# Three stage joints in a fused transformer kernel: inputs fetched in the stage before, a store wait moved, region fills split over two queues

## What is computed

```python
def reference(...):
    x = x + ssm_block(layernorm(x))       # silu/sigmoid gate, scan over 1024 steps, rms norm, projection
    x = x + moe(layernorm(x))             # 8 experts, 2 for each token, 256 -> 512 -> 256, relu
    qkv = einsum('bsi,oi->bso', layernorm(x), W_qkv); Q, K = rope(Q), rope(K)
    attn = softmax(where(causal, Q @ K.T / sqrt(16), -inf)); x = x + (attn @ V) @ W_o.T   # 16 heads of 16
    x = x + moe2(layernorm(x))            # 16 experts, 2 for each token, and a shared one
    return x
```

## Time and profile before

| | us |
|---|---|
| runs, median (lowest to highest, 3) | 1679.52 (1676.56 to 1681.55) |
| the profiled execution | 1680.78 |
| its span, first to last instruction | 1679.1 |
| PE busy in the span | 1507.6 (90%) |
| DVE busy | 1016.9 (61%) |
| ACT busy | 735.6 (44%) |
| POOL busy | 575.4 (34%) |

### The profile page before, as it was taken

The page is one execution under the profiler, slowest core; times in us unless marked ns, Lnnn a source line. Parts: engine busy times, 40 slices in busy tenths (PEclk is TensorE's granted clock), DMA queues, the critical chain, the costliest instruction groups (busy, mean ns, idle before and its releaser), DMA issues. The chain is left out here.

```text
span 1679.1 us, 31220 instructions
## 1 busy us (share of the span) xinstructions
PE 1507.6 (90%) x9903; PEld 1136.5 (68%) x9903; DVE 1016.9 (61%) x3465; ACT 735.6 (44%) x1537; POOL 575.4 (34%) x995
## 2 busy tenths in 40 slices
PE   5999999983999999599599999999999597489988
PEld 3777777772999999456366666666666376368877
DVE  3345555443344444389598888888887275545558
ACT  3444444420222222245157777777777232244420
POOL 4123333344222222135623322333223164635520
PEclk9999999985999999799799999999999887789999
DMA  7001111013877777567956666666661485745556
GB/s 229 1 26 42 48 46 51 33 51 112 236 210 210 216 214 210 171 229 244 218 72 92 92 91 96 96 92 92 92 92 42 131 261 161 175 133 158 160 163 195
DMA packets 150592, 221.74 MB, mean 132 GB/s; under 512 B 23648, under 2 KB 98144, under 8 KB 150304
## 3 DMA queue, kind: packets, MB, share of 16 engines
q1 hardware_dynamic: 128672, 170.59, 44.1%
q0 software_dynamic: 13344, 36.55, 6.2%
q10 hardware_dynamic: 8416, 12.60, 2.5%
HBM read 141.16 MB, written 78.25 MB: 131 GB/s over the span
## 5 line engine op out<-in xcount | busy, mean ns | idle before, releaser
L1958 ACT ACTIVATE t_probs<-t_ps_st 128x512 f32<-128x512 f32 x576 | 313.2, 597 | 125.2 <-PE t_ps_st L2010 122.7
L1939 DVE CUSTOM_DVE_ANT_0 whole_sum<-t_ps_s,t_later 128x512 bf16<-128x512 f32 (+3 forms) x512 | 285.6, 587 | 16.6 <-PE t_ps_s L1996 14.6
L1915 POOL TENSOR_SCALAR_AFFINE_SELECT t_probs<-t_probs 128x128 f32<-128x128 f32 x512 | 137.4, 300 | 333.1 <-ACT t_probs L1958 331.4
L1996 PE MATMUL t_ps_s<-t_ks,t_qs 96*128 96x512 f32 (+3 forms) x768 | 247.6, 362 | 0.5 <-ACT t_neg_max L1951 0.5
L2010 PE MATMUL t_ps_st<-t_qs,t_ks 128*128 128x512 f32 (+3 forms) x768 | 242.7, 365 | 1.1 <-ACT t_probs L1958 0.8
L2010 PEld LDWEIGHTS t_ps_st<-t_qs,t_ks 128*128 128x128 f32 x768 | 136.8, 189 | 74.1 <-ACT t_probs L1958 40.7
L1939 DVE CUSTOM_DVE_ANT_0 whole_sum<-t_ps_s,t_later,t_first_max 128x512 bf16<-128x512 f32 (+3 forms) x256 | 140.5, 549 | 47.7 <-PE t_ps_s L1996 47.7
L2025 PE MATMUL t_ps_o<-t_probs,t_vs 128*17 128x256 f32 (+1 forms) x2560 | 154.9, 361 | 0.5 <-ACT whole_sum L1965 0.5
L1996 PEld LDWEIGHTS t_ps_s<-t_ks,t_qs 96*128 96x128 f32 x768 | 138.7, 190 | 17.6 <-DVE t_first_max L1939 1.3
L1381 PE MATMUL m_ps_h<-m_xt,m_w_t 128*128 128x128 f32 x1136 | 140.1, 277 | 0.0
L1351 POOL DMA_INDIRECT outputs_dram<-m_y,m_place x71 | 68.1, 959 | 208.2 <-DVE m_place L1426 200.5
(11 more groups left out here) (324 smaller groups left out, 2697.3 us busy)
## 6 DMA issues: line engine op xcount, KB each, us to landing
m_w_t<-in_w_dram SPq DMA_DIRECT2D x71, 512.0 KB, 4.4
t_qs<-qkt_dram SPq DMA_DIRECT2D x124, 128.0 KB, 5.2
t_ks<-qkt_dram SPq DMA_DIRECT2D x124, 128.0 KB, 5.6
m_x_t<-gathered_dram SPq DMA_DIRECT2D x79, 128.5 KB, 2.1
m_x_t<-gathered_dram SPq DMA_DIRECT2D x71, 129.0 KB, 2.2
d_ye<-outputs_dram SPq DMA_DIRECT2D x8, 1024.0 KB, 8.0
qkt_dram<-d_hi ACTq DMA_DIRECT2D x32, 256.0 KB, 5.1
qkt_dram<-d_lo SPq DMA_DIRECT2D x32, 256.0 KB, 6.7
```

Of the source, the lines that this page charges most:

```text
L1915: nc.gpsimd.affine_select(out=diag, in_=diag, compare_op=ALU.is_ge, fill=0.0, base=0, pattern=[[1, P]], channel_multiplier=-1).then_inc(ma ...
L1939: nc.vector.tensor_tensor_reduce(out=seen[:, (NP * p + x) % (RS + 1), 0:keys], in0=bank_of(p, x)[:, 0:keys], in1=masks, scale=1.0, scalar= ...
L1958: nc.scalar.activation(probs[:, p % 2, i // NST, base:base + STC], ps_st[(NX * p + i) % RT][:], ACT.Exp, scale=HD ** -0.5).then_inc(exp_re ...
L1996: nc.tensor.matmul(bank_of(p, x)[:, 0:keys], q[0:MAX_ROW, head, qc * P:(qc + 1) * P], k[0:MAX_ROW, head, k0:k0 + keys], start=True, stop=T ...
```

## The change

1. The weights, the rope table and x of the first two groups are loaded by SP at the end of its list in the experts' stage (`load_qkv_start`). Their buffers are made before that stage; rope lies in the last rows of `total`.
2. In `project_qkv` SP no longer waits for the stores of q and k. That wait stands in `attention` in two places: before ACT's first exponential and before SP's load of pair 8. The semaphores live outside the stages.
3. The loads of the first pair of heads move from ACT, tick 8, to SP, tick 6.
4. For group 7, DVE and not POOL adds the second two sums (`add_last`).
5. Six leading dummy matmuls in attention become three.
6. In `back` the fills of the first eight regions stay with SP, the other eight go to ACT, after its exponentials (`close_regions`).

```diff
                 fetch(t)
+            fetch_next(sp)
 
...
 
-def project_qkv(nc, sb, pb, sem, c, x_dram, outputs, kept, total, sum_dram, w_qkv_dram, rope_dram, qkt_dram, vs, fetch):
+def group_rows(dram, g):
+    return dram[bass.ts(g, 4 * P), :].rearrange("(j p) n -> p j n", p=P)
+
+
+def load_qkv_start(eng, c, total, x1_dram, w, w_qkv_dram, rope, rope_dram):
+    eng.dma_start(w[:], w_qkv_dram.rearrange("(k p) n -> p k n", p=P)).then_inc(c["w_loaded"], 16)
+    eng.dma_start(rope, rope_dram[0:SEQ, :].rearrange("(c p) d -> p c d", p=P)).then_inc(c["rope_loaded"], 16)
+    for g in range(2):
+        eng.dma_start(total[:, 4 * g:4 * (g + 1), :], group_rows(x1_dram, g)).then_inc(c["x_loaded"][g], 16)
+
+
+def project_qkv(nc, sb, pb, sem, c, x_dram, outputs, kept, total, sum_dram, w, rope, qkt_dram, vs, fetch):
 
...
                 wait(sp, x2_ready, g - 1)
-                sp.dma_start(total[:, J * g:J * (g + 1), :], rows(x_dram, g)).then_inc(x_loaded[g % 2], 16)
+                if g >= 2:
+                    sp.dma_start(total[:, J * g:J * (g + 1), :], rows(x_dram, g)).then_inc(x_loaded[g % 2], 16)
                 sp.dma_start(ye[:, g % 2].rearrange("p j i n -> p j (i n)"),
...
             load(0)
-            sp.dma_start(w[:], w_qkv_dram.rearrange("(k p) n -> p k n", p=P)).then_inc(w_loaded, 16)
-            sp.dma_start(rope, rope_dram[0:SEQ, :].rearrange("(c p) d -> p c d", p=P)).then_inc(rope_loaded, 16)
             load(1)
             for tick in range(groups + 3):
                 if tick < SPILL // J:
                     store_sum(tick)
                 if live(tick + 2):
                     load(tick + 2)
+                if tick == groups - 2:
+                    for s in range(2):
+                        sp.wait_ge(qk_stored[s], 32 * NB)
+                    fetch(sp)
                 if live(tick - 3):
                     store_lo(tick - 3)
             sp.wait_ge(sum_stored, 16 * (SPILL // J))
-            for s in range(2):
-                sp.wait_ge(qk_stored[s], 32 * NB * (groups // 2))
 
...
                     add_turned(tick - 2, 0)
-                    add_turned(tick - 2, 1)
+                    if tick - 2 < groups - 1:
+                        add_turned(tick - 2, 1)
 
...
 
+            def add_last():
+                g, s = groups - 1, (groups - 1) % 2
+                dve.wait_ge(by_ready, 8 * g + 8)
+                dve.wait_ge(hi_ready, NB * g)
+                dve.wait_ge(lo_ready, NB * g)
+                nc.vector.tensor_tensor(qk[:, 2, :], by[:, s, 1, 0, :], by[:, s, 1, 1, :], ALU.subtract).then_inc(late_sum, 1)
+                nc.vector.tensor_tensor(qk[:, 3, :], by[:, s, 1, 2, :], by[:, s, 1, 3, :], ALU.add).then_inc(late_sum, 1)
+
             def rest(g, n):
...
                         rest(tick - 3, n)
+                if tick == groups + 1:
+                    add_last()
                 if live(tick):
...
             def round_qk(g, n):
-                act.wait_ge(sum_ready, NB * g + n + 1)
+                if g == groups - 1 and n >= 2:
+                    act.wait_ge(late_sum, n - 1)
+                else:
+                    act.wait_ge(sum_ready, NB * g + n + 1)
                 if n == 0:
...
             for tick in range(groups + 2):
-                if tick == groups:
-                    for s in range(2):
-                        act.wait_ge(qk_stored[s], 32 * NB)
-                    fetch(act)
                 if live(tick):
...
                 wait(sp, st_done, NX * (p - RINGQ) + NX)
+                if p == PAIRS:
+                    for s in range(2):
+                        sp.wait_ge(c["qk_stored"][s], ALL_STORED)
                 load_heads(sp, p, qs[p % RINGQ], ks[p % RINGQ], qkt_dram, qk_loaded[p % RINGQ])
...
                     wait(act, av_done, NR * (p - 1))
+                if p == 0 and i == 0:
+                    for s in range(2):
+                        act.wait_ge(c["qk_stored"][s], ALL_STORED)
                 base = (i % NST) * STC
...
 
-            for i in range(6):
+            for i in range(3):
                 keep_busy(i, 4 * P)
...
 
+    def close_regions(eng, first, last):
+        eng.wait_ge(list_ready, 1)
+        for e0 in range(first, last, 4):
+            rows = nc.values_load_multi_w_load_instructions(
+                pad_row[0:1, e0:e0 + 4], engines=[eng.engine], min_val=0, max_val=(E - 1) * CAP + TOK,
+                skip_runtime_bounds_check_because="a row is a region's start and a count of at most all tokens")[1]
+            for at in rows:
+                eng.dma_start(gathered[bass.ds(at, P), :], zeros[:]).then_inc(padded, 16)
+
     def coming_down(tick):
...
                 sp.dma_start(gathered[E * CAP + e * P:E * CAP + (e + 1) * P, :], zeros[:]).then_inc(padded, 16)
-            sp.wait_ge(list_ready, 1)
-            for e0 in range(0, E, 4):
-                rows = nc.values_load_multi_w_load_instructions(
-                    pad_row[0:1, e0:e0 + 4], engines=[sp.engine], min_val=0, max_val=(E - 1) * CAP + TOK,
-                    skip_runtime_bounds_check_because="a row is a region's start and a count of at most all tokens")[1]
-                for at in rows:
-                    sp.dma_start(gathered[bass.ds(at, P), :], zeros[:]).then_inc(padded, 16)
+            close_regions(sp, 0, E // 2)
             sp.wait_ge(padded, 32 * E)
...
             nc.scalar.activation(soft_best[:], soft_best[:], ACT.Exp).then_inc(exp_ready, 1)
+            close_regions(act, E // 2, E)
             act.wait_ge(exp_ready, 2)
...
             c["m0_stored"] = [sem(f"m0_stored{s}") for s in range(RING)]
+            c["qk_stored"] = [sem(f"d_qk_stored{s}") for s in range(2)]
+            c["x_loaded"] = [sem(f"d_x_loaded{s}") for s in range(2)]
+            c["w_loaded"], c["rope_loaded"] = sem("d_w_loaded"), sem("d_rope_loaded")
             kept = router_keep(first, "r0_", E0)
             with ExitStack() as weights:
                 wsb = lambda n, s, d=FP32: weights.enter_context(nc.sbuf_tensor(n, s, d))
                 w2_sb, b1_turned, b2_sb = wsb("w2_sb", [P, H0 // P, E0 * DM]), wsb("b1_turned", [P, E0 * (H0 // P)]), wsb("b2_sb", [P, E0 * DM])
                 fetch = lambda eng: load_moe0(nc, eng, moe0_loaded, b1_turned, b1, w2_sb, w2, b2_sb, b2)
                 phase(front, c, x_in, w_in, w_abc, w_out, norm_w, x1_dram, gate_w, gate_b, gathered[0], kept, E0, fetch)
+                total = whole.enter_context(nc.sbuf_tensor("whole_sum", [P, NT, DM], FP32, side="right"))
+                vs = ahead.enter_context(nc.sbuf_tensor("t_vs", [P, BATCH, TPB, NH, HD + 1], FP32, side="right"))
+                q_first, k_first = (ahead.enter_context(nc.sbuf_tensor(n, [P, 2, SEQ], FP32R, side="right")) for n in ("t_qs0", "t_ks0"))
+                w_qkv_sb = ready.enter_context(nc.sbuf_tensor("w_qkv", [P, KD, 3 * DM], FP32, side="right"))
+                rope_sb = total[:, NT - 1, :].rearrange("p (c d) -> p c d", d=2 * HD)
                 phase(run_wide_experts, c, E0, gathered[0], outputs[0], kept, w1, b1_turned, w2_sb, b2_sb,
-                      (moe0_loaded, 16 * (H0 // P + 2)))
-
-            total = whole.enter_context(nc.sbuf_tensor("whole_sum", [P, NT, DM], FP32, side="right"))
-            vs = ahead.enter_context(nc.sbuf_tensor("t_vs", [P, BATCH, TPB, NH, HD + 1], FP32, side="right"))
-            q_first, k_first = (ahead.enter_context(nc.sbuf_tensor(n, [P, 2, SEQ], FP32R, side="right")) for n in ("t_qs0", "t_ks0"))
-            phase(project_qkv, c, x1_dram, outputs[0], kept, total, x2_dram, w_qkv, rope, qkt_dram, vs,
+                      (moe0_loaded, 16 * (H0 // P + 2)),
+                      lambda eng: load_qkv_start(eng, c, total, x1_dram, w_qkv_sb, w_qkv, rope_sb, rope))
+
+            phase(project_qkv, c, x1_dram, outputs[0], kept, total, x2_dram, w_qkv_sb, rope_sb, qkt_dram, vs,
                   lambda eng: load_heads(eng, 0, q_first, k_first, qkt_dram, first_loaded))
+            ready.close()
 
```

18 lines of the change are left out of this document (9 added, 9 removed).

## The result

The changed kernel takes 1660.34 us (median of 5, 1659.04 to 1671.27), the kernel before 1679.52 us; the ratio is 0.9902 with a 95% interval of 0.9876 to 0.9928. Two more comparisons of the same pair, taken later with the experiments, gave 0.9884 (0.9856 to 0.9913) and 0.9895 (0.9870 to 0.9920). The change is worth some 16 to 20 us; 18.0 were forecast.

The account below looks back on a forecast made before the run. TensorE is busy 90% of the span and stands still at three stage joints, where the last arrival sets the time; gains of 5.9 + 9.0 + 2.6 + 0.5 = 18.0 us give 1661.5 us, range 1655.5 to 1668.5.

Parts of the forecast that it names:

- Joint one: Experts to projection: loads issued early let the first add of expert outputs start sooner, gain 5.9 us (4.1 to 8.1).
- Joint two: Projection to attention: shorter chain through the engines and no wait for the stores' landing, gain 9.0 us (6.8 to 9.8).
- SyncE's last store is issued by 814.1: Projection's end: last store issued by 814.1 after VectorE's last remainder at 813.4; with 1.5 us of barriers attention opens at 815.6.
- VectorE's pair: Projection's tail: VectorE's two sums of group 7 run from 808.9 to 810.7, one add contended and one free.
- Dummies: Attention's opening: three fewer dummy matmuls at 0.44 us per pass, gain 2.6 us, or 0 if the faster clock comes later.
- Fills: Region ends before the second expert stage: two queues issue at most 5.2 us sooner, gain 0.5 us (−1.0 to 5.2).
- Signs: Named in advance: last store some 5 us earlier, first piece 4.6 us after opening, expert stage at most 1 us earlier.
- Head loads as a bill: Attention's opening: head loads queue behind draining stores, delaying the row of maxima; up to 3 us lost, 1664.5 us, chance 0.17.
- Issue bound: Region-end fills: bound by issue, so two queues bring 4.7 us more, 1656.8 us, chance 0.09.
- First joint gives nothing: Projection: bound by loads, so the earlier start is waited away by group 2 or 3; 1667.4 us, chance 0.07.
- Chain doesn't shorten: Projection's tail: ScalarE's lateness is due to group 4's stores; 9.0 us becomes 4.6, total 1665.9 us, chance 0.06.
- Slower through the clock: Attention's opening: TensorE stays at 1.2 GHz through the lead steps, costing 18.2 us; 1686.5 us at 25 us, chance 0.03.

Follow-up runs that it names:

- e1: Changed kernel with x, weights and rotation table issued only when the projection opens, as before; 1676.38 us beside 1670.62 us for the changed kernel.
- e7: Changed kernel with attention's three dropped dummy matmuls put back, six in all; first score piece 7.2 us after attention opens, no total time given.
- e2: Changed kernel with only the eight head loads back on ScalarE's queue, two ticks later; 1670.69 us against 1670.62 us for the changed kernel.
- a1: Changed kernel run again without edit; 1665.34 us beside 1683.00 us for the kernel before, ratio 0.9895.
- b0: Kernel before the change, profiled again without edit; first score piece 7.9 us after attention opens, no total time given.
- e5: Changed kernel with all region-end fills back on SyncE's queue; next expert stage opens 19.3 us behind the first fill, no total time given.
- e9: Changed kernel plus six unused matmuls in the projection's opening and ten at its tail, attention's three dummies removed; 1667.80 us beside 1665.34 us for the changed kernel.

## Why the prediction was right, and where its sizes were off

By distances the change is worth 5.7 (A: 34.1 to 28.4) + 7.1 (C: 18.9 to 11.8, the mean of the seven kernels whose second joint is untouched) + 2.2 (D) + 1.2 (E) = 16.2 us, against 18.0 in the sum. The medians say 17.7 to 19.2, the ratios 16.5 to 19.6, with intervals from 12 to 24 us. That the time of 1660.34 lies so near 1661.5 is partly luck: two of its five executions took 1667.64 and 1671.27, and the term that was too large by 1.9 us is made up by something that I can't name. The last stage, some 2 us shorter on average, is a candidate, but the second expert stage is 1.2 us longer on average, and two profiles of the kernel before are too few to show either.

**Joint one** (forecast 5.9, measured 5.7 by A, 5.8 by e1's time): right in mechanism and size. The fastest load of expert outputs lands in 5.4 us now, where I had worked out 5.1 from 6.6 less the x in front of it. That the projection passes the earlier start on was argued from VectorE's full windows; B of e1 shows it.

**Joint two** (forecast 9.0, measured 7.1). The chain itself came out as computed. On the clock of the kernel before, that is less the 1.35 us by which the last bias is later, ACT's last rounding ends at 811.7 (forecast 811.7) and VectorE's last remainder at 813.4 (forecast 813.4). The step that failed is the one behind it, "SyncE's last store is issued by 814.1": I gave the store 0.7 us behind the remainder, and it took 2.6 (814.76 to 817.31), because the last two stores needed 1.55 and 1.52 us where the first needed 0.52. ACT's four took 4.09, not the 2.5 of my value, and more than its other end of 3.7. This store term is the whole miss of 1.9 us:

```profile
L1539 SPq DMA_DIRECT2D qkt_dram<-d_lo x4: 518/1046/1551, 813.0 to 815.8; - x4
...
L1690 ACTq DMA_DIRECT2D qkt_dram<-d_hi x4: 526/840/1769, 812.4 to 814.7; - x4
```

These are the last four stores on either queue (issue time min/median/max in ns, first and last start). In the kernel before, SyncE's last four and the window around them were:

```profile
L1527 SPq DMA_DIRECT2D qkt_dram<-d_lo x4: 517/518/518, 812.7 to 816.9; - x4
812.00:818.00 6.00, 0.00 (x0) 0.00 (x0) 4.51 (x4) 1.89 (x3) 3.47 (x3) 0.50 1.05 401
```

So a full DMA share alone does not make an issue long: at 1.05 they took 0.52 us each. They stood 0.8 to 1.7 us apart. Now the first three start 0.6 us apart and the fourth as soon as the queue is free, beside four from ACT, at shares of 0.90 to 1.02, and the third and fourth are long. ACT's four in a row were so before, too: 0.53, 0.61, 1.12 and 1.44 us are in the 3.82 of the earlier trace rows. The change packed SyncE's stores together, and the forecast kept their old price. What holds up the issue of such a row of stores no run shows.

Two slips lie inside the forecast of this joint. It priced VectorE's pair at 1.8 us (808.9 to 810.7) and called that one contended and one free add, which by its own values, 1.755 and 0.68, is 2.4; the pair took 2.1, and the remainders behind it 2.5 instead of 2.7, so the end still fitted. And its lower bound of 6.8 does not follow from its two losses, 1.7 and 1.2 us, which together leave 6.1. In parts: heads off ACT 2.0 (forecast 2.1), landing 4.0 (forecast 4.6, the gain if only that goes), the pair of sums 1.3 (forecast the 2.3 that are left of 9.0); together 7.3, so the parts add up to the whole within 0.2.

**Dummies** (forecast 2.6, measured 2.2): right in mechanism. The granted clock comes up 3.4 to 5.9 us behind attention's opening, in different executions; the forecast took the 3.6 of the earlier trace rows. Where it comes up by 3.6 us, the price is the forecast's: D is 7.2 with six dummies (before, e7) and 4.5 to 4.6 with three (e2, a1). In the others more passes run at 1.2 GHz: 7.9 with six (b0) and 5.0 to 5.7 with three. **Fills** (forecast 0.5, measured 1.2): the size is inside its bounds, the reason right, since the issue's length and the opening are not tied.

**Signs.** Of those named in advance, two came out otherwise: the last store is issued 3.4 us earlier (819.33 before, 815.96 now on the same clock), not some 5, and the first piece stands 5.2 us behind the opening on average, not 4.6. The expert stage's opening behind the fills is at the edge, 1.1 to 1.2 us earlier where no more than 1 was named.

**Rivals.** *Head loads as a bill*: F is 482.7 to 482.9 in every changed kernel with three or six dummies, and 483.0 before, and in the lead steps TensorE waits 0.5 us for ACT and 0.4 us for VectorE, never for the row's transfer. *Issue bound*: out, by e5. *First joint gives nothing*: out, by e1. *Chain doesn't shorten*: out, by e2 and by the rounding of group 6, which no longer waits. *Slower through the clock*: the mechanism exists and e9 shows it, one step further on than the change goes. With three dummies the clock is up at the first piece (the window 824.40 to 828.00 above); with none it is not, and then the lead steps cost 1.5 us, far from the 18 us that this rival needed.
